# Attention heads taken in pairs through scores, softmax, transposes and values, in a fused attention and spiking feed-forward kernel

## What is computed

```python
q = (src @ Wq + bq).reshape(B, nb, bs, H, dk)      # H = 8 heads, bs = 64 tokens, dk = 128
k = (src @ Wk + bk).reshape(B, nb, bs, H, dk)
v = (src @ Wv + bv).reshape(B, nb, bs, H, dk)
scores = jnp.einsum('bnqhd,bnkhd->bhnqk', q, k) * dk ** (-0.5)
probs = jax.nn.softmax(scores, axis=-1)
out = jnp.einsum('bhnqk,bnkhd->bnqhd', probs, v).reshape(B, S, D)
return out @ Wo + bo
...
h = jnp.square(jax.nn.relu(jnp.einsum('bsd,fd->bsf', x, W_fc)))   # 4096 wide
y = jnp.einsum('bsf,df->bsd', h, W_proj)                          # then 5 spiking steps on y
...
x = x + _L0_attn_ref(_layernorm(x, axis=-1), ...)
x = x + _L0_ffn_ref(_layernorm(x, axis=-1), ...)
```

## Time and profile before

| what | value |
|---|---|
| median of 3 runs | 717.28 us (717.11 to 857.81) |
| the profiled execution: its own time | 718.44 us |
| its span on the slowest core (core 3) | 716.9 us; the 8 cores 713.9 to 716.9 |
| mean granted TensorE clock | 0.997 to 0.999 on the 8 cores |
| PE busy | 703.1 us, 98% of the span |
| DVE busy | 394.4 us, 55% |
| ACT busy | 173.3 us, 24% |

### The profile page before, as it was taken

How to read it: one execution, slowest core, us unless ns; L and a number is a source line. 1 busy time by engine, 2 the same in 40 slices (tenths; PEclk the granted TensorE clock), 3 DMA queues, 4 the chain that set the end, 5 groups by cost and what they waited for, 6 DMA issues and landing times.

```text
span 716.9 us, 10967 instructions; the slowest of 8 cores (713.9 to 716.9 us)
## 1 busy us (share of the span) xinstructions
PE 703.1 (98%) x3804; PEld 325.0 (45%) x3804; DVE 394.4 (55%) x669; ACT 173.3 (24%) x330; POOL 49.5 (7%) x96
## 2 busy tenths in 40 slices
PE   7999999999999999998999999999999999999996
PEld 3544444444444444443444444444444444444444
DVE  5325766786587476425855225865225766221476
ACT  3553330550262044130002331001332001332000
POOL 2212110121004200100000000000000000000000
PEclk9999999999999999999999999999999999999999
DMA  8998987688659995697172002172002141100011
GB/s 178 212 148 153 140 149 198 119 198 215 150 143 190 221 239 88 154 208 167 48 215 89 0 1 59 42 192 91 30 0 54 36 148 59 59 0 1 30 45 44
DMA packets 31013, 80.95 MB, mean 113 GB/s; under 512 B 5616, under 2 KB 5872, under 8 KB 30192
## 3 DMA queue, kind: packets, MB, share of 16 engines
q0 software_dynamic: 12960, 31.46, 26.6%
q1 hardware_dynamic: 15552, 40.39, 20.2%
q10 hardware_dynamic: 2448, 8.40, 3.0%
HBM read 82.33 MB, written 16.78 MB: 138 GB/s over the span
## 4 chain that ended last, share of the span: by engine, by line
PE 89%; DMA 8%; DVE 1%; issue 1%; POOL 0%; DVEq 0%; POOLq 0%
PE ps_m L397 28%; PE ps_y L466 28%; PE ps_m L344 13%; PE ps_m L370 8%; PE ps_m L384 8%; DMA w_sb<-Wpr 4%; DMA wq_sb<-Wq 4%; PE ps_y L419 1%; PE ps_y L447 1%; DVE acc_sb L710 1%; PE ps_m L473 1%; PE ps_t L431 0%; DVE acc_sb L707 0%; POOL w_sb L801 0%; PE ps_t L326 0%
## 5 line engine op out<-in xcount | busy, mean ns | idle before, releaser
L397 PE MATMUL ps_m<-xn2t,w_sb 128*128 128x512 bf16 x1024 | 224.5, 379 | 0.0
L466 PE MATMUL ps_y<-w_sb,h_sb 128*128 128x512 bf16 (+1 forms) x1024 | 218.4, 376 | 2.0 <-DMA w_sb<-Wpr 2.0
L466 PEld LDWEIGHTS ps_y<-w_sb,h_sb 128*128 128x128 bf16 x1024 | 100.1, 98 | 119.9 <-issue 2.5
L397 PEld LDWEIGHTS ps_m<-xn2t,w_sb 128*128 128x128 bf16 x1024 | 99.0, 98 | 116.9
L552 ACT ACTIVATE h_sb<-ps_m 128x512 bf16<-128x512 f32 x128 | 76.4, 597 | 266.5 <-PE ps_m L397 266.5
L700 DVE TENSOR_TENSOR h_sb<-h_sb 128x512 bf16<-128x512 bf16 x128 | 53.3, 423 | 121.9 <-ACT h_sb L552 121.9
L710 DVE SCALAR_TENSOR_TENSOR acc_sb<-ps_y,acc_sb 128x1024 bf16<-128x1024 f32 (+2 forms) x72 | 78.6, 1092 | 7.9 <-DVE acc_sb L710 0.5
L344 PE MATMUL ps_m<-xnt,wk_sb 128*128 128x512 bf16 x248 | 58.6, 379 | 0.4 <-DMA wk_sb<-Wk 0.4
L370 PE MATMUL ps_m<-wv_sb,xnt 128*128 128x512 bf16 x256 | 58.2, 380 | 0.0
L344 PE MATMUL ps_m<-xnt,wq_sb 128*128 128x512 bf16 x240 | 56.9, 380 | 1.3 <-DMA wq_sb<-Wq 1.1
L384 PE MATMUL ps_m<-wo_sb,attn_sb 128*128 128x512 bf16 x256 | 55.9, 379 | 0.0
(11 more groups left out here) (63 smaller groups left out, 375.3 us busy)
## 6 DMA issues: line engine op xcount, KB each, us to landing
xr<-x SPq DMA_DIRECT2D x32, 512.0 KB, 7.5
xl<-x SPq DMA_DIRECT2D x96, 128.0 KB, 5.0
w_sb<-Wfc POOLq DMA_DIRECT2D x32, 256.0 KB, 10.0
x<-xr ACTq DMA_DIRECT2D x16, 512.0 KB, 6.9
out<-xr POOLq DMA_DIRECT2D x12, 512.0 KB, 3.0
w_sb<-Wpr POOLq DMA_DIRECT2D x16, 256.0 KB, 36.2
xn2t<-blk SPq DMA_DIRECT2D x64, 64.0 KB, 2.0
w_sb<-Wpr POOLq DMA_DIRECT2D x4, 1024.0 KB, 19.3
```

The lines of the kernel that those rows point to most:

```text
L397: m = E.matmul(bank(key)[:], w1_sb[fc // 4][:, k0:k0 + 128], tokens(xn2t, c, 0, 4), start=(c == 0), stop=(c == 7))
L466: return E.matmul(out, h_sb[fc][:, tt * 128:(tt + 1) * 128], w2_sb[fc // 4][:, k0:k0 + n], start=(fc == 0), stop=(fc == 31))
```

## The change

Two heads (a pair j, heads 2j and 2j+1) go through every step together. `scores(b, j)` writes 16 matmuls, one head into each of the two banks of `ps_y0`, and signals once. DVE and ACT handle both heads with one instruction of twice the columns: maximum, subtraction, exponential, sum, reciprocal, product and `p_copy`. `turn_p` makes four transposes and `values` 16 matmuls, for both of which PE signals once. Only `value_copy` stays one for each head, two in a row. `e_sb` and `pt_sb` have one buffer of twice the size instead of two.

The pieces stand at other slots: scores at 0, 4, 8, 12 in every block; transposes at 4j+5 (block 0: 4j+13); values three slots later, which is 8, 12, 16, 20 (block 0: 16, 20, 24, 28). So block 0 has 4 slots with scores alone and 4 with values alone, and blocks 1 to 3 have 2 with scores alone, 2 with both and 2 with values alone. The LayerNorm units of blocks 0 to 2 stand one slot later than before. On DVE `softmax_scale` now stands behind the LayerNorm pieces of its slot.

```diff
-def turn_p_head(b, s):
-    h = (s - (11 if b == 0 else 3)) // 2
-    return h if b >= 0 and s % 2 == 1 and 0 <= h < 8 else None
+def scores_pair(b, s):
+    return s // 4 if b >= 0 and s % 4 == 0 and s < 16 else None
+def turn_p_pair(b, s):
+    j, rest = divmod(s - (13 if b == 0 else 5), 4)
+    return j if b >= 0 and rest == 0 and 0 <= j < 4 else None
+def values_pair(b, s):
+    return turn_p_pair(b, s - 3)
...
-    first, apart = {-1: (3, 3), 0: (14, 4)}.get(b, (2, 4))
+    first, apart = {-1: (3, 3), 0: (15, 4)}.get(b, (3, 4))
...
-        def scores(p, h):
-            n = 8 * p + h
-            E.wait_ge(*emptied(("q", p, h)))
-            E.wait_ge(*emptied(("k", p, h)))
-            if n >= 2:
-                E.wait_ge(free_s, n - 1)
-            for bl in range(8):
+        def scores(p, j):
+            n = 4 * p + j
+            for h in (2 * j, 2 * j + 1):
+                E.wait_ge(*emptied(("q", p, h)))
+                E.wait_ge(*emptied(("k", p, h)))
+                if n > 0:
+                    E.wait_ge(free_s, n)
+                for bl in range(8):
...
-            for i in range(2):
+            for i in range(4):
                 m = E.transpose(ps_t[:, i * 128:(i + 1) * 128],
...
-            if n > 0:
-                E.wait_ge(free_v, n)
-            for bl in range(8):
+            if p + j > 0:
+                E.wait_ge(free_v, 8 * p + 2 * j)
+            for h in (2 * j, 2 * j + 1):
+                for bl in range(8):
...
-                if (h := values_head(b, s)) is not None:
-                    value_copy(b, h)
+                if (j := values_pair(b, s)) is not None:
+                    value_copy(b, 2 * j)
+                    value_copy(b, 2 * j + 1)
...
-                if b >= 0 and s % 2 == 1 and s < 16:
-                    softmax_scale(b, s // 2)
                 if (i := ln_unit(b, s, LN_SCALE)) is not None:
                     ln_scale(i)
                 if b >= 0 and (i := ln_unit(b, s, LN_BLOCKS)) is not None:
                     ln_blocks(i)
                 if (i := ln_unit(b, s, LN_STATS)) is not None:
                     ln_stats(i)
+                if s > 0 and (j := scores_pair(b, s - 1)) is not None:
+                    softmax_scale(b, j)
```

More of the change, by code:

```diff
@@ L141, in turn_order @@
                 keys.append(("x", i))
-            if (h := turn_p_head(b, s)) is not None:
-                keys.append(("pt", b, h))
+            if (j := turn_p_pair(b, s)) is not None:
+                keys.append(("pt", b, j))
     return {k: n for n, k in enumerate(keys)}
@@ L182, in build_nc @@
     attn_sb = at("attn_sb", ATTN_AT, 4096, BF16)
-    p_sb = [at(f"p_sb_{i}", WORK + 57344 + 512 * i, 256, BF16) for i in range(8)]
+    p_sb = [at(f"p_sb_{i}", WORK + 57344 + 1024 * i, 512, BF16) for i in range(4)]
     bo_sb = at("bo_sb", WORK + 61440, 1024, F32)
@@ L200, in build_nc @@
     xn = [at(f"xn_{i}", WORK + 90112 + 2048 * i, 1024, BF16) for i in range(2)]
-    e_sb = [at(f"e_sb_{i}", WORK + 94208 + 1024 * i, 256, F32) for i in range(2)]
-    pt_sb = [at(f"pt_sb_{i}", WORK + 96256 + 512 * i, 256, BF16) for i in range(2)]
+    e_sb = at("e_sb", WORK + 94208, 512, F32)
+    pt_sb = at("pt_sb", WORK + 96256, 512, BF16)
     acc_sb = at("acc_sb", WORK + 94208, 1024, BF16)
@@ L410, in main @@
                 up_group(key)
[L412 to L424 removed]
+        def scores(p, j):
[6 more added lines that the diff above has]
+                for bl in range(8):
+                    s0 = (h % 2) * 512 + (bl % 4) * 64
+                    m = E.matmul(
+                        ps_s[(bl // 4) * 64:(bl // 4) * 64 + 64, s0:s0 + 64],
+                        q_sb[:, h * 512 + bl * 64:h * 512 + (bl + 1) * 64],
+                        k_sb[:, h * 512 + bl * 64:h * 512 + (bl + 1) * 64],
+                        start=True, stop=True)
@@ L433, in turn_p, with values @@
             m.then_inc(full_t, 1)
[L435 to L439, removed]
-            if n > 0:
-                E.wait_ge(free_v, n)
-            for bl in range(8):
[L443 to L448, removed]
+        def values(p, j):
+            E.wait_ge(free_t, turn_no[("pt", p, j)] + 1)
+            if j % 2 == 0:
+                E.wait_ge(*emptied(("v", p, 3, j // 2)))
+            if p + j > 0:
+                E.wait_ge(free_v, 8 * p + 2 * j)
+            for h in (2 * j, 2 * j + 1):
+                for bl in range(8):
+                    kb = (bl % 2) * 64
+                    p0 = (h % 2) * 256 + (bl % 4) // 2 * 128 + (bl // 4) * 64
+                    o0 = (bl % 2) * 512 + (h % 2) * 256 + (bl // 2) * 64
+                    v0 = (bl // 2) * 1024 + h * 128
+                    m = E.matmul(ps_v[:, o0:o0 + 64], v_sb[kb:kb + 64, v0:v0 + 128],
+                                 pt_sb[kb:kb + 64, p0:p0 + 64], start=True, stop=True)
@@ L487, in tensor_program @@
                     turn_x(i)
[L488 to L491, removed]
-                if (h := values_head(b, s)) is not None:
-                    values(b, h)
+                if (j := scores_pair(b, s)) is not None:
+                    scores(b, j)
+                if (j := turn_p_pair(b, s)) is not None:
+                    turn_p(b, j)
+                if (j := values_pair(b, s)) is not None:
+                    values(b, j)
                 if b == -1 and s < HALVED:
@@ L553, in main, with exps @@
             m.then_inc(emptied(key)[0], 1)
[L555 to L558, removed]
+        def exps(p, j):
+            E.wait_ge(free_s, 4 * p + j + 1)
+            E.activation(e_sb[:], e_sb[:], ACT.Exp).then_inc(ac_exp, 1)
         def store_x2(p, tt):
@@ L594, in scalar_program @@
                     main(key)
-                if b >= 0 and s % 2 == 0 and s < 16:
-                    exps(b, s // 2)
+                if (j := scores_pair(b, s)) is not None:
+                    exps(b, j)
                 if b >= 0 and (i := ln_unit(b, s, LN_RSTD)) is not None:
@@ L739, in vector_program @@
             for s, key in enumerate(keys):
[L740 to L743, removed]
-                if b >= 0 and s % 2 == 1 and s < 16:
-                    softmax_scale(b, s // 2)
+                if (j := scores_pair(b, s)) is not None:
+                    softmax_shift(b, j)
+                if (j := turn_p_pair(b, s)) is not None:
+                    p_copy(b, j)
                 if (i := ln_unit(b, s, LN_SCALE)) is not None:
```

62 lines of the change are left out of this document (30 added, 32 removed).

## The result

The changed kernel takes **712.3 us** (median; 711.65 to 713.11) against 717.3: a ratio of 0.9928, 95% interval 0.9917 to 0.9939. It is 0.7% faster, clear of noise but less than 2%. The forecast was 712.1. (Medians and ratios leave out single executions in which one die ran at a lower clock, such as the 857.81 us of the table; a ratio is one of means, so it can differ by a little from that of the medians beside it.)

The account below looks back on a forecast made before the run. PE was taken as the bound, busy 703.1 of 716.9 us. A gain of 5.35 less 0.15 at block 3's end made 5.2 us: 717.28 - 5.2 = 712.1 us, range 710.4 to 715.6.

Parts of the forecast that it names:

- slot prices of before: PE time beyond a 1.726 us output group: scores alone 0.353, scores and values 0.573, values alone 0.323, two transposes 0.123.
- x and y: Cost on PE of eight more scores (x) and eight more values (y) in one batch: 0.29 together, gain 5.35 us.
- The starts: Start times of the eight small matmuls on PE's timeline, read as x + y of 0.25, gain 6.0 us.
- leaving cost: Assumed for PE at the end of a small batch: leaving costs what entering costs, 0.095 us, subtracted from the hold times.
- the formula: PE's stream in the four attention blocks gets shorter by 10.0 - 16(x and y summed) us.
- "side by side" bound: Two halves of the array work at once on small matmuls: half of 0.43, gain 6.5, time 710.9 us; chance 0.17.
- one after another: Small matmuls on PE run singly, 0.027 us each: x + y = 0.43, gain 3.1 us.
- both dearer cases: Second eight matmuls on PE cost 0.43 to 0.48: gain 2.3 to 3.1, time 714.3 to 715.1 us; chance 0.22.
- Two copies ahead of block 3's output groups: End of block 3: output groups wait for the second value copy, PE loses about 0.15 us.
- The transposing DMAs: Head of block 1: DMAs start about 2.6 us later but land before q needs them, slack 0.3 to 2.2, no wait.
- End of block 0: Later LayerNorm pieces may delay slot 30's copy by at most 1.24 us; 1.5 us are there, so no loss.
- Softmax chain, weights: Attention softmax: about 7 us DVE work within some 9, no PE wait; feed-forward weight transfers move with PE, losing no gain.

Follow-up runs that it names:

- singles experiment: Changed kernel with every DVE and ACT softmax instruction and the copy of turned probabilities made for one head again, TensorE still in pairs: 713.14 us, ratio 0.9940.
- the two "apart" ones: Changed kernel with the first head's values one slot earlier: 716.27 us; the same with the second head's scores also one slot later: 720.33 us.
- full-array one: Changed kernel with the same small matmuls at the same places in the full array's shape, block separation left out: 713.31 us, ratio 0.9938.
- values apart: Changed kernel with the values of each pair's first head one slot earlier than those of its second: 716.27 us, ratio 0.9972.
- everything apart: Changed kernel with first heads' values one slot earlier and second heads' scores one slot later, DVE and ACT still in pairs: 720.33 us, ratio 1.0029.

## Why the prediction was right

**The bound and the place of the gain.** PE's stream was named as the only thing that moves the time, and the places of small work as the part of it that shrinks. The singles experiment shows that DVE's and ACT's share is nothing that the blocks show, the two "apart" ones that the time follows the entries and batches, and the full-array one that the entry comes with the small shape. DVE's own saving was oversized: 14 us forecast, 9.8 measured, which costs the time nothing.

**The slot prices of before** (0.353, 0.573, 0.323, 0.123) held: they gave 3.3 us for the values apart (3.3 measured). For everything apart the time was forecast at 719.0; 1.0029 of the 717.3 us of before is 719.4, with 0.3 us more in the blocks than the prices give.

**x and y.** Forecast 0.165 + 0.125 = 0.29; measured 0.40 - 0.26 = 0.14 and 0.34 - 0.22 = 0.12, so 0.26. The starts (0.25) were the better reading, and the subtraction of an entry's cost as the leaving cost was a little too careful. With 0.26 the formula gives 10.0 - 4.2 = 5.8 us. The blocks without the new delays (45.82 for block 1, 40.64 for block 3) give 1.62 + 3 x 1.42 = 5.9. From two sizes a line can be drawn: scores hold 0.12 + 0.0175 for each matmul, values 0.10 + 0.015. That lies near the "side by side" bound of 0.0135 for each and well below the 0.027 of one after another, so both dearer cases are out. The Trainium skill, "TensorEngine Tiling (Array Packing)", section "Key Properties", states that different tiles load weights and multiply in parallel; by these rows (0.0175 and 0.015 against 0.0135) it holds nearly.

By these lines most of the 5.8 us is not the entry, which the prediction named first. There are 22 fewer entries at 0.095, 2.1 us; 16 fewer batches of scores and 16 fewer of values, whose fixed parts of 0.12 and 0.10 make 3.5 us; and 0.2 us from transposes in half as many places. What the fixed part is stays open. It may be the cost of leaving a small shape, which the prediction put at 0.095; that it is absent in the full array's shape fits this and does not prove it. Scores hold the same 0.40 ahead of values (139.11 to 139.51), the other small shape, as ahead of a group.

**Two copies ahead of block 3's output groups.** Forecast 0.15, measured 0.1 at the first output group; moving the values by a slot took it away.

**The transposing DMAs: the step that failed.** "Nothing, but close" was wrong: every core waits, 0.3 to 1.1 us. A wait of q for DMA at the head of block 1 was one of the prediction's own signs of being wrong. The start was forecast well: 7.9 us behind the values of slot 28 (110.34 - 102.42) against 5.35 before plus 2.6. What was off is the term behind it. I took 9.99 us for sixteen issues from one core of before; on its 8 cores they take 10.0 to 10.6, and after 11.14 on core 0 (11.1 to 11.6 on the 8 cores). The last DMA is issued at 120.88 and takes 3.36 us to land, inside the 2.0 to 3.9 that the prediction allowed, and the q group starts 0.24 later, at 124.48 instead of 123.98. An estimate from these numbers: with an issue of 9.99 us the same landing would let q start at 123.3, 0.6 us ahead of the need; with 10.5 at 123.9, barely in time. So the term that failed is the length of the issue, and the wait needs both it and the later slot. The longer issue isn't tied to the new slot, since it is 10.0 to 12.4 with the LayerNorm back, too. On core 0 a typical issue is as long as before (0.59 us), but the longest is 1.35 us where it was 1.03. Why stays open; other DMAs (the stores of `xr` from 114.92 on) run beside it, as they did before.

**End of block 0.** No wait there, as forecast: block 0 has its full 1.62 us. The copy of slot 30 runs from 110.12 to 110.77, and the second output group, 1.73 us behind the first (109.68), needs its bank at 111.4. (The 110.65 that the prediction took for the output groups of before is the row of the chain; on the timeline they start at 110.49. Its slack of 1.5 is 1.4 then, and the 6.4 us left for block 0's pieces are 6.2, which its sum of 6.29 fits as well.)

**Softmax chain, weights.** No wait of PE for DVE or ACT in any block. The 2.0 us wait for the last `Wpr` weights, which I took to move along unchanged, is 0.2 to 2.0 us on six cores of before and 0.6 on one core of after, 0.2 to 1.5 on all cores with everything apart, and 0 to 1.3 in the others. It varies by core and execution by more than the smaller effects here. On the slowest core of before it is 2.0 us and on that of after none, which is nearly all of the 2.2 us that the part behind block 3 lost; that the change caused it is not shown.

**The sum.** 5.2 us were forecast and 5.0 measured (5.2 in the blocks), by two misses that cancel: 0.5 more from x and y, about 0.5 lost to the DMAs. The mechanism was right and the size of the gain near; that the number came out to 0.2 us is luck.

## What to carry to other kernels

Here TensorE was the bound, and the engines beside it gave nothing by doing their work in fewer instructions. What paid was fewer and larger batches of small-shaped matmuls: count the changes of shape, and the batches too. A new slot for a piece of work far from TensorE still moves every transfer behind it: take the slack from the worst core and the longest landing, not from one row, and leave some over (the longest issue of sixteen on any core before was 10.6 us, after it was 11.6). A hold time divided by its matmuls is not the price of one more: two batch sizes are needed to part the fixed cost from the slope, and with only one the starts of the single matmuls gave the best hint here (0.25 against 0.26 measured).

## What the runs showed of the hardware

From the batches of 8 (before) and of 16 (after): a batch of 64-wide matmuls behind a full group costs an entry of 0.095 us, then 0.10 to 0.12 us, then 0.015 (values, 64 rows) or 0.0175 us (scores, 64 columns of weights) for each matmul. In the full array's shape the same number of matmuls of 64 columns cost 0.029 us each, for 16 and for 32, with no entry and no fixed part. At 8 matmuls, an estimate by these lines that no run tried, the full array would be the cheaper (0.23 against 0.35 for scores alone); at 16 they are near each other (0.46 against 0.495 for scores alone, 0.93 against 0.84 for both), and it leaves out the separation that attention needs here. I had allowed for up to 0.055 us for each matmul, the spacing of the transposes, and it was half of that.
